# A state-space, attention and mixture-of-experts layer on one core: the end of attention reordered, and the routing moved by a period

## The reference, cut to what matters

```python
h = concatenate([_L0_tok_ref(x, ...), txt], axis=1)          # 8 x 384 x 512
h = h + attention(layernorm(h))                              # 16 heads, 4 KV heads, rope, HD 32
h = h + moe(layernorm(h))                                    # below

logits = x @ gate_w.T                                        # 64 experts
topk_w, topk_i = top_k(softmax(logits), 6)
pos    = rank of each (token, expert) among all tokens, in token order
valid  = pos < 64                                            # capacity
y      = down(silu(gate(x)) * up(x)) of each expert's slots, weighted, summed over the 6
y + shared                                                   # a shared expert of 704 on every row
```

## Time and profile before

| quantity | value |
| --- | --- |
| time, median of 3 runs | 1470.17 us (1469.13 to 1474.4) |
| the profiled execution | 1472.85 us, its span 1471.1 us |
| PE busy | 1248.9 us, 85% of the span |
| PE weight loads | 795.6 us, 54% |
| DVE busy | 757.1 us, 51% |
| POOL busy | 498.9 us, 34% |
| ACT busy | 419.8 us, 29% |
| DMA | 239.82 MB, mean 163 GB/s |

### The profile page before, as it was taken

How to read it: one execution, slowest core, us unless ns; L and a number is a source line. 1 busy time by engine, 2 the same in 40 slices (tenths; PEclk the granted TensorE clock), 3 DMA queues, 4 the chain that set the end, 5 groups by cost and what they waited for, 6 DMA issues and landing times. The chain is left out here.

```text
span 1471.1 us, 23499 instructions
## 1 busy us (share of the span) xinstructions
PE 1248.9 (85%) x9192; PEld 795.6 (54%) x9192; DVE 757.1 (51%) x1667; ACT 419.8 (29%) x695; POOL 498.9 (34%) x453
## 2 busy tenths in 40 slices
PE   5263778889898999999987879999999999969995
PEld 5252443445454454646444868666666666646662
DVE  7993566666776867786854352232233222312321
ACT  2221214444444443535354421111111111111110
POOL 0000101111213434343466374334444434343444
PEclk9597779999999999999999899999999999989998
DMA  3033231312425151524271484799999999888993
GB/s 113 1 75 85 53 72 42 84 42 71 122 60 133 36 136 22 151 42 127 45 230 43 133 277 61 221 312 298 309 327 343 302 329 349 264 259 298 332 284 41
DMA packets 141109, 239.82 MB, mean 163 GB/s; under 512 B 61368, under 2 KB 81480, under 8 KB 141000
## 3 DMA queue, kind: packets, MB, share of 16 engines
q1 hardware_dynamic: 117160, 214.10, 45.8%
q0 software_dynamic: 23840, 24.23, 9.2%
HBM read 175.59 MB, written 38.90 MB: 146 GB/s over the span
## 5 line engine op out<-in xcount | busy, mean ns | idle before, releaser
L1993 POOL DMA_INDIRECT out_rows<-mo_y,mo_scatter_half x128 | 180.9, 1413 | 253.9 <-DMA out_rows<-mo_y,mo_scatter_half 183.7
L1355 DVE TENSOR_REDUCE at_maxes<-at_ps 128x1 f32<-128x384 f32 x384 | 195.3, 552 | 63.3 <-PE at_ps L916 56.6
L1122 ACT ACTIVATE bulk<-at_ps 128x1152 f32<-128x1152 f32 x128 | 144.6, 1129 | 272.2 <-PE at_ps L883 250.5
L1616 POOL DMA_INDIRECT slot_table<-at_toki,at_si x144 | 143.6, 997 | 105.7 <-DVE at_maxes L1355 74.0
L70 PE MATMUL mo_ps<-arena_view,arena_view 128*117 128x384 f32 (+1 forms) x864 | 168.8, 344 | 1.1 <-PEq L570 1.1
L70 PEld LDWEIGHTS mo_ps<-arena_view,arena_view 128*117 128x117 f32 (+1 forms) x864 | 146.5, 179 | 14.6 <-issue 14.5
L916 PE MATMUL at_ps<-late_view,late_view 128*128 128x384 bf16 x384 | 117.0, 355 | 35.9 <-DVE at_maxes L1355 18.1
L874 PE MATMUL at_ps<-arena_view,arena_view 128*128 128x512 f32 (+1 forms) x576 | 115.6, 352 | 3.8 <-ACT arena_view L1209 2.3
L874 PEld LDWEIGHTS at_ps<-arena_view,arena_view 128*128 128x128 f32 x576 | 90.7, 193 | 36.9 <-issue 22.4
L916 PEld LDWEIGHTS at_ps<-late_view,late_view 128*128 128x128 bf16 x384 | 31.2, 98 | 145.4 <-DVE at_maxes L1355 108.5
L883 PE MATMUL at_ps<-arena_view 97*128 97x384 f32 x384 | 97.8, 364 | 9.6 <-DMA arena_view<-at_mrow 5.1
(11 more groups left out here) (222 smaller groups left out, 1774.4 us busy)
## 6 DMA issues: line engine op xcount, KB each, us to landing
bulk<-in_L_ffn_w_gate SPq DMA_DIRECT2D x32, 704.0 KB
bulk<-in_L_ffn_w_up SPq DMA_DIRECT2D x32, 704.0 KB
late_view<-in_L_ffn_w_gate SPq DMA_DIRECT2D x32, 704.0 KB
late_view<-in_L_ffn_w_up SPq DMA_DIRECT2D x32, 704.0 KB
arena_view<-arena_view SPq DMA_DIRECT2D x96, 192.0 KB
late_view<-in_L_ffn_w_down SPq DMA_DIRECT2D x32, 512.0 KB
bulk<-in_L_ffn_w_down SPq DMA_DIRECT2D x32, 512.0 KB
out_rows<-at_hr SPq DMA_DIRECT2D x8, 768.0 KB, 3.8
```

The lines of the kernel that those rows point to most:

```text
L1122: A.activation(PT[:, N % RING, :, :], ps[:, 0:NT, 0:SEQ], ACT.Exp, scale=float(HD) ** -0.5)\
L1355: V.tensor_reduce(maxes[:, half, s, h:h + 1], ps[:, raw_bank(a, u), 0:SEQ], AX.X, ALU.max, negate=True)\
L1616: G.indirect_dma_start(slot_table, bass.IndirectOffsetOnAxis(ap=si[:, e % 2, m:m + 1], axis=0), toki[:, e % 2, m // TOPK:m // TOPK + 1], N ...
L1993: G.indirect_dma_start(acc_halves, bass.IndirectOffsetOnAxis(ap=scatter_half[:, half, 2 * p + e:2 * p + e + 1], axis=0), y[:, p % 2, e, co ...
```

## The change

In the steady periods (those with a next sequence) the router logits of d go from PE's slot 4 to slot 6, and the routing of that sequence follows one period later, as sequence e: routing steps in slots 1 to 4 on DVE, gate exponentials in slot 2 on ACT, places in slot 4 on PE and in slot 5 on POOL, slots in slot 7 on DVE. In the last period both sequence 4 (as e) and 5 (as d) are routed; the output projection of sequence 6 runs in slots 5 to 10 over banks 6, 5 and 7, its residuals in slots 7, 9 and 11, its statistics in 11, its inverse deviation on POOL in 12, and its normalisation on ACT in 13. The scatters of 4 go from slots 2 to 7 to slots 4 to 9, and 12 (not 10) of those of 5 to slots 9 to 12. Behind the loop turn_x2 and logits of sequence 6 come first, the rest follows in a new order, and the splits of the down weights come earlier. The store of rows is split in rows and scores.

```diff
@@ tables @@
+        LAST_OUT_SLOT = {5 + n: 2 * n for n in range(2 * NT)}
+        LAST_OUT_BANK = (6, 5, 7)
+        LAST_RESIDUAL_SLOT = {7: 0, 9: 1, 11: 2}
+        LAST_DIVIDED = {13: -4, 15: -3}
+        ROUTE_SLOT = {2: (5,), 3: (6,), 4: (7,)}
+        LAST_ROUTE_SLOT = {0: (4, 5), 1: (6,), 3: (7,)}
...
-        SCATTERED_LAST = 10
+        SCATTERED_LAST = 12
@@ PE, a slot @@
-                    if prev2 and n == 4:
+                    if prev3 and n == (4 if nxt else 2):
+                        places(e)
+                    if prev2 and n == (6 if nxt else 4):
                         logits(d)
-                    if prev2 and n == 6:
+                    if prev2 and not nxt and n == 6:
                         places(d)
...
+                    if b == B - 1 and n in LAST_OUT_SLOT:
+                        project_out(c, LAST_OUT_SLOT[n], LAST_OUT_BANK[LAST_OUT_SLOT[n] // 4])
@@ PE, behind the loop @@
+            for k in range(KC):
+                turn_x2(B - 2, k, (7, 6))
+            for i in range(4):
+                project_out(B - 1, i, 0)
+            logits(B - 2)
+            for i in range(4, 12):
+                project_out(B - 1, i, i // 4)
             shared_unit(0)
-            for k in range(NT):
-                for i in range(4 * k, 4 * k + 4):
-                    project_out(B - 1, i, k)
-                turn_x2(B - 2, k)
+            places(B - 2)
             shared_unit(1)
-            turn_x2(B - 2, 3)
             shared_unit(2)
...
@@ ACT, a slot and behind the loop @@
-                    if prev2 and n == 4:
+                    if prev2 and n == (6 if nxt else 4):
                         logits_copied(d)
...
+                    if prev3 and n == (2 if nxt else 1):
+                        gate_exponentials(e)
...
+                        if n == 13:
+                            normalised2(B - 2)
                         if n == 14:
                             shared_rows_hi(0)
-
-            for G in range(NKV * B - 4, NKV * B - 1):
-                out_hi(G)
-            normalised2(B - 2)
+                        if n in LAST_DIVIDED:
+                            out_hi(NKV * B + LAST_DIVIDED[n])
...
+            for m in range(2 * KC, PIECES):
+                weights_hi(m)
@@ DVE, a slot @@
-                    if prev3 and n == 1:
-                        slots(e)
+                    if prev3 and nxt and n == 1:
+                        routing(e, 4)
...
-                    if prev2:
-                        routing(d, n)
+                    if prev3:
+                        for step in (ROUTE_SLOT if nxt else LAST_ROUTE_SLOT).get(n, ()):
+                            routing(e, step)
+                    if prev3 and n == (7 if nxt else 4):
+                        slots(e)
+                    if prev2 and not nxt:
+                        for step in {4: (4,), 5: (5,), 6: (6, 7)}.get(n, ()):
+                            routing(d, step)
@@ POOL, a slot and behind the loop @@
-                    if prev2 and n == 7:
+                    if prev3 and n == (5 if nxt else 3):
+                        places(e)
+                    if prev2 and not nxt and n == 7:
                         places(d)
...
-                    if b == B - 1 and 2 <= n < 8:
-                        scatter(e, 3 * (n - 2), 3 * (n - 1))
-                    if b == B - 1 and 10 <= n < 10 + SCATTERED_LAST // 2:
-                        scatter(d, 2 * (n - 10), 2 * (n - 9))
-
-            for N in range(NKV * B - 4, NKV * B - 1):
-                out_lo(N)
-            inverse_deviation2(B - 2)
+                    if b == B - 1 and 4 <= n < 10:
+                        scatter(e, 3 * (n - 4), 3 * (n - 3))
+                    if b == B - 1 and n == 12:
+                        inverse_deviation2(B - 2)
+                    if b == B - 1 and 9 <= n < 9 + SCATTERED_LAST // 3:
+                        scatter(d, 3 * (n - 9), 3 * (n - 8))
+                    if b == B - 1 and n in LAST_DIVIDED:
+                        out_lo(NKV * B + LAST_DIVIDED[n])
```

168 lines of the change are left out of this document (100 added, 68 removed).

## The result

The changed kernel is slower by 0.8%: its median is 1483.44 us over 17 runs (1472.02 to 1492.38), that of the kernel before 1469.13 us over 17 runs (1463.89 to 1480.07), and the ratio is 1.0081 with a 95% interval of 1.0053 to 1.0110. Against the recorded median of 1470.17 that is 1482.1 us. Two later jobs, on two different chips, measured the same kernel at 1.0013 (0.9983 to 1.0043) and 1.0000 (0.9964 to 1.0035). So the loss is clear in the first comparison and not to be told from no change in the other two; the experiments have to explain both.

A forecast was written before the change was run, and what follows sets the result against it. With PE busy 99.29 of 100 us in the untouched expert phase, the shift of its first matmul decides. Period 2 −1.9, steady +9.6, last +10.2, tail −14.6 sum to +3.3 us: 1473.5 us, range 1463 to 1483.

The forecast's parts named there:

- rival 1: Last period: POOL is no queue, inverse deviation of sequence 6 ready by 790; 1461.3 us, chance 0.17.
- Period 2: Period b = 2, now without routing: PE's waits for mask and rope_sum go, −1.9 us (bounds 0 and −2.5).
- Steady periods: Periods 3 to 6: placing ahead of rope_sum(2), slots(e) ahead of row maxima, +2.4 us each, +9.6 in all (4.8 to 14.4).
- Last period: Period 7: POOL's inverse deviation of sequence 6 comes late behind scatters and ACT waits; +10.2 us (+5 to +13).
- inverse deviation ready at 800.6: Last period, POOL: 755.3 + 27 scatters (35.4) + placing 4.0 + out_lo 1.0 + waits 3.8 + operation 1.1.
- ACT waits for it, and the exponentials of 14 and 15 are queued behind: Last period, ACT: normalised2(6) waits about 10 us for POOL, so the last values end at 812.9, against 802.8.
- The residual's wait of 3.41 us: Last period: three banks for sequence 6's output projection remove PE's wait for DVE's residual; gain swallowed by ACT's wait.
- The row of before with 5.66 us: Last period, ACT's wait before slot 14's exponential, perhaps an instruction fetch; would fall into ACT's wait for POOL, sum unchanged.
- rival 3: Last period: down-weight halves on DVE hold POOL up for their whole length, 5.6 us more; 1479.1 us, chance 0.10.
- Rival 2: Steady periods: POOL's placing block starts at 616.7, not 614.2; 4.9 us a period, 1483.5 us, chance 0.20.
- Tail: Last values to the experts phase: four PE waits go (−15.6 us), turn_x2 waits about 1; −14.6 us (−10 to −18).
- The expert phase simply moves: Experts phase, untouched by the diff: starting x us earlier or later shifts the end by x; own change 0.

The follow-up runs named there:

- e1: The changed kernel with no edit, run again for a second trace; ratio to before 1.0013 (0.9983 to 1.0043).
- f1: The changed kernel with no edit, run side by side with its halves on one chip; ratio to before 1.0000, median 1460.64 us.
- f4: Repeat of e3: the changed kernel with slots(e) ahead of q_lo on DVE in steady periods; ratio to before 0.9994 (0.9963 to 1.0026).
- e5: The changed kernel with the edits of e3 and e8 together; ratio to before 0.9984 (0.9951 to 1.0017).
- e3: The changed kernel with slots(e) of steady periods moved ahead of q_lo on DVE; ratio to before 0.9996 (0.9965 to 1.0027).
- e4: The changed kernel with POOL's inverse deviation of sequence 6 in slot 9 instead of 12 of the last period; ratio to before 1.0012.
- e2: The changed kernel with routing in steady periods put back as before, the end as changed; ratio to before 0.9903 (0.9867 to 0.9938).
- the end alone: The kernel of e2, steady routing as before and only the end of attention and tail changed; ratios to before 0.9903 and, repeated, 0.9905 (1448.52 us).
- job 3: The job on one chip that ran the kernel before, e5, e6, e7 and e8, without the changed kernel; ratios to before 0.9984, 0.9929, 0.9987, 1.0055.
- e6: e2 with POOL's inverse deviation of sequence 6 in slot 10 instead of 12; ratio to before 0.9929 (0.9895 to 0.9963).
- e7: e2 with slots(4) of the last period in slot 4 instead of slot 1 on DVE; ratio to before 0.9987 (0.9958 to 1.0016).
- e8: e4 with six instead of twelve scatters of sequence 5 ahead of the last out_lo; ratio to before 1.0055 (1.0021 to 1.0088).
- jobs 2 and 4: Two jobs on different chips, each with the kernel before: one ran e1 to e4, the other f1, f4 and repeats of e2 and e7; changed kernel 1.0013 and 1.0000.

## Why the prediction was right, and where it was not

The forecast was +3.3 us with a range of 1463 to 1483. The first comparison gives 1482.1 on its scale, inside the range but near its end, and on the side of "slower by over 0.5%", which had 0.30, where "no change" had 0.53. The two later jobs give +2 and 0 us. Part of what should have shown it wrong did come: in the first trace ACT did not wait for the inverse deviation at all (the sign of rival 1, by another cause), and the experts phase did not simply move.

- **Period 2**, -1.9: measured -1.8. Right.
- **Steady periods**, +9.6: measured +7.6 in the first trace and 8.9, 8.4 against that trace of before in e1 and f1. The size was right, the reason half. Of the +2.4 us a period that were forecast, the place of slots(e) gives 1.6 at the first row maximum, since the block took the 1.83 us of the tail and not the 2.6 of slot 1; the 0.8 us more in slot 1 were one conversion (L1443) that took 0.95 us there and 0.18 here. Half of what the order costs is the clock (4.2 of 8.9 us in the means above), and the sum had no term for it. f4 and e5 show that most of the loss can stay with the block moved away, e3 that it need not. That +9.6 came out near the 7.6 to 8.9 is thus in part luck.
- **Last period**, +10.2: measured +16.2 in the first trace, +7.9 in e1 and +9.1 in f1. The step "inverse deviation ready at 800.6" was right to 0.1 us, counted from the period's start. So close a hit is luck: the first scatter came 18.1 us after the start and not 17.3, and the placing took 5.3 us and not 4.0, but the waits were 1.8 us (for the scores) and not 3.8. The step "ACT waits for it, and the exponentials of 14 and 15 are queued behind" was right in e1 and f1 (11.12 and 13.62 us) and did not come into play in the first trace. The residual's wait of 3.41 us went as forecast. (Unrounded the sum gives +10.0, not +10.2.) What the sum did not have is the 14.54 us of the first trace ahead of the exponential of slot 13. The row of before with 5.66 us and the same releaser was read as something that would fall into ACT's wait; it is the other way round: it came ahead of it and was longer. The prediction offered the rule of the Trainium skill on instruction fetch for that row (page "Runtime: NRT & Kernel Launch", section "🔬 Instruction fetch mechanics"). No run supports it: in the trace of after the blocks of 16 KB on the instruction queue started to move at 785.5 and 825.9, for 1 us each, and one of 8 KB on a second such queue at 813.6; between 786.6 and the end of the wait at 812.5 none moved. What PE stood for is open.
- **Rival 1** (POOL is no queue) falls by e1, f1 and e4, **rival 3** (the weight halves hold the scatters up) by the cadence: 27 scatters of the changed kernel took 27.3 us and 7.6 of gaps, 1.29 each, a bit under the 1.31 of the sum. Against 0.97 us for an undisturbed scatter these 27 took 1.1 us more in all, beside eight operations on the down weights of 7.9 us together. The rule of the Trainium skill (page "SBUF — State Buffer", section "🔬 SBUF: two separate sides") would have asked for up to the whole of these; the trace again shows a small part. **Rival 2** (placing late on POOL) falls too: the block began at 613.65, and out_lo ahead of it half a microsecond earlier than assumed.
- **Tail**, -14.6: measured -14.6 in the first trace, but not by the terms of the sum, so the exact number is luck. The four waits went, 15.6 us, but PE's idle time fell by 11.1 only, since 2.79 us for issue and smaller ones are new; the other 3.5 us are the higher clock, for which the sum had no term. (It also counted the old tail as 121 us, to the end of the work ahead of PE's last wait of 1.06; to the first matmul it is 122.0.) e1 and e2 show 99.9 us. That is 7.5 less than the first trace: 4.3 us less busy time at a clock of 1.00, the rest fewer waits. It is no proof that the order gives 22 us, since the 122.0 come from a trace that has the standing PE: the time of the end alone fell by 14.
- **"The expert phase simply moves"** does not hold for a single execution: its length is 534 to 549.5 us over the traces, and 549.5, 547.1 and 537.2 in three of the changed kernel, see below. The +3.2 us of the first pair of traces are no evidence on the change.

So the term that was off is the last period's, by 6 us in the first trace (16.2 for 10.2), and what took its place there is the standing PE. Why the first 17 runs show +11.9 us on the recorded median's scale and the others +2 and 0 is shown only as far as one trace can: it has 7 to 8 us in the last period that e1 and f1 have not, and these are the standing PE. That all 17 runs had it isn't shown. A rival stands untested, that the loss goes with the chip: the kernel before took 1469.13 and 1469.16 us in the two jobs whose traces have the standing PE (the first comparison and job 3), 1459.85 and 1463.84 in the other two, and the changed kernel was not run in job 3.

The version that beats both is the end alone: 0.9903 and 0.9905 in two jobs, 14 us; it was not run where PE stands, only its variants e6 (0.9929) and e7 (0.9987).

## What to carry to other kernels

Where a change is several that were put in together, run the halves: here the end gave 14 us, and the moved routing, which was put in with it, took all of it back, in the last period and in the steady ones. On an in-order queue that is behind, moving one item ahead helps its reader and makes the next reader pay; what counts is when the queue begins (e4, e7). And where the engine's clock differs between executions, taking a block of work out may leave a stretch nearly as long as it was in one trace (f4, 317.8 us) and not in the next (e3, 311.5): take more than one trace, and read busy and idle time apart.

## What the runs showed of the hardware

- **PE's signals can come 3 to 19.5 us late with nothing in the records to account for it.** The matmuls have their rows, the semaphore that they raise comes late, and ACT and DVE wait for "remote". It is in the traces of before (5.66 us in the last period, 9.21 in the tail), after (5.52 and 14.54) and of all four kernels of job 3 (the longest 9.0 to 19.5 us, mostly at the same places in e5 and e8), and in none of the eight traces of jobs 2 and 4. It seems to go with the chip or the job, not with the kernel. Its cause is open.
- **The experts phase varies by 15 us between executions of one kernel.** Waits of PE for the transposed rows (releaser, then the sum, the number and the longest of them) in before, f4 and e3:

```profile
PE mo_ps L1838 <- DVE mo_xgT L1961: 12.8, 4, 11.3
```
```profile
PE mo_ps L1902 <- DVE mo_xgT L2025: 1.7, 2, 0.8
```
```profile
PE mo_ps L1902 <- DVE mo_xgT L2025: 12.5, 3, 11.3
```

  e3 and f4 are the same kernel, 549.4 and 534.0 us: one wait of 11.3 us, met in some executions and not in others, is most of the difference. Over all traces these waits sum to 10.2 to 12.8 us where the phase takes 546.0 to 549.5, and to 1.7 to 5.2 where it takes 534.0 to 540.8. The runs of one kernel in one job spread over 13 to 28 us (the two named with the result apart), and differences of 5 us between two traces must be read by stretches and not by their ends.
- **A granted clock at its lower level for a few microseconds in a period** lengthened PE's busy time over periods 3 to 6 by 5.8 us between two executions of one kernel (281.69 us at 0.98 in e3, 287.50 at 0.96 in f4), of 7 us between the two stretches.
